# Selective scan on one core: moving two of eight multiplies by the step size from VectorE to GpSimd, through copies by ScalarE

## What is computed

```python
proj = x @ W_x                                  # delta_raw, B_ssm, C_ssm
delta = softplus(delta_raw @ W_dt + b_dt)
A = -exp(A_log)                                 # (128, 16)
dA = exp(einsum('bld,dn->bldn', delta, A))
dBx = einsum('bld,bln->bldn', delta * x, B_ssm)

def step(h, inp):
    dA_t, dBx_t, C_t = inp
    h = dA_t * h + dBx_t
    y_t = einsum('bdn,bn->bd', h, C_t)
    return (h, y_t)
```

## Time and profile before

| what | value |
|---|---|
| median of 3 runs | 2394.18 us (2393.65 to 2394.51) |
| time of the profiled execution | 2391.51 us |
| its span, first to last instruction | 2389.5 us |
| granted TensorE clock over the span | 0.921 |
| busy: TensorE, VectorE, ScalarE, GpSimd | 1911.1, 1571.5, 1375.2, 1019.3 us |

### The profile page before, as it was taken

One profiled execution on the slowest core, in us unless ns is written; L12 is line 12 of the kernel. 1 busy time (PEld: TensorE's weight loads), 2 busy tenths in 40 slices (PEclk: granted clock), 3 DMA queues, 4 the chain that ended last, 5 costly groups with the idle time before them and its releaser, 6 DMA issues. The chain is left out here.

```text
span 2389.5 us, 36303 instructions
## 1 busy us (share of the span) xinstructions
PE 1911.1 (80%) x11731; PEld 865.0 (36%) x11731; DVE 1571.5 (66%) x2373; ACT 1375.2 (58%) x2286; POOL 1019.3 (43%) x1118
## 2 busy tenths in 40 slices
PE   4457886377774765899999999999999966599997
PEld 2113332243453421344444444444444422222222
DVE  4979995786447856777777777777777635511112
ACT  2446662343333334677666676666666533599995
POOL 0156663244004521466666666666666631500001
PEclk9769998589896987999999999999999988899999
DMA  2000000000000001111111111111111100512110
GB/s 87 0 14 0 0 0 0 1 1 1 0 1 0 1 1 52 47 55 54 53 54 56 56 56 56 56 56 56 56 56 56 50 24 8 124 41 52 46 50 36
DMA packets 71431, 84.45 MB, mean 35 GB/s; under 512 B 20545, under 2 KB 44033, under 8 KB 71169
## 3 DMA queue, kind: packets, MB, share of 16 engines
q1 hardware_dynamic: 66224, 79.80, 11.5%
q10 hardware_dynamic: 5040, 2.56, 0.4%
HBM read 71.95 MB, written 9.57 MB: 34 GB/s over the span
## 5 line engine op out<-in xcount | busy, mean ns | idle before, releaser
L1638 DVE SCALAR_TENSOR_TENSOR fu_kv<-fu_ps_kv,fa_vec,fu_kv 128x511 f32<-128x511 f32 x366 | 253.2, 741 | 5.6 <-ACT fu_kv L1568 4.0
L2032 ACT ACTIVATE rt_p<-rt_ps_s 128x1024 f32<-128x1024 f32 x256 | 240.3, 1042 | 25.3 <-PE rt_ps_o L1977 16.5
L1716 POOL TENSOR_TENSOR fu_p<-fu_p 128x768 f32<-128x768 f32 x64 | 116.2, 1816 | 295.2 <-PE fu_ps_n L1413 290.8
L1383 PE MATMUL fu_ps_s<-fu_qn,fu_kn 64*128 64x512 f32 (+3 forms) x1024 | 190.0, 468 | 6.1 <-ACT fu_p L1550 5.5
L1618 DVE TENSOR_REDUCE fu_nm<-fu_ps_m 128x2 f32<-128x1024 f32 x64 | 78.4, 1225 | 176.5 <-PE fu_ps_m L1406 176.5
L602 POOL TENSOR_TENSOR scan_hC<-scan_h,scan_c 128x1024 f32<-128x1024 f32 x64 | 150.7, 2354 | 82.9 <-DVE scan_h L582 82.9
L1413 PE MATMUL fu_ps_n<-fu_p,fu_vt 128*64 128x512 f32 (+3 forms) x1024 | 166.1, 445 | 0.0
L527 PE MATMUL scan_ps_y<-scan_hC,w_ident 128*128 128x512 f32 x256 | 130.3, 632 | 40.9 <-POOL scan_hC L602 24.3
L582 DVE TENSOR_TENSOR_SCAN scan_h<-scan_dA,scan_ps_b 128x1024 f32<-128x1024 f32 x64 | 146.4, 2287 | 2.2
L1977 PE MATMUL rt_ps_o<-rt_p,rt_va 128*32 128x512 f32 x1024 | 137.2, 608 | 10.0 <-ACT rt_p L2032 8.1
L1441 PE MATMUL fu_ps_kv<-w_XN,fa_wp 128*128 128x512 f32 x244 | 122.8, 626 | 17.3 <-DVE fu_cr L1611 15.3
(11 more groups left out here) (353 smaller groups left out, 5071.3 us busy)
## 6 DMA issues: line engine op xcount, KB each, us to landing
fu_rb<-rms_rows SPq DMA_DIRECT2D x256, 128.0 KB, 3.0
fu_ro<-rms_rows SPq DMA_DIRECT2D x128, 128.0 KB, 3.0
ra_stackq<-rope_parts SPq DMA_DIRECT2D x168, 32.0 KB
ra_stackk<-rope_parts SPq DMA_DIRECT2D x168, 32.0 KB
w_X<-in_xT SPq DMA_DIRECT2D x4, 512.0 KB
fa_wp<-in_wp SPq DMA_DIRECT2D x8, 256.0 KB
fu_cr<-ncum_rows SPq DMA_DIRECT2D x128, 3.0 KB
rope_parts<-rp_hi SPq DMA_DIRECT2D x16, 128.0 KB, 2.9
```

The costliest lines, as they stand in the source:

```text
L1383: pe.matmul(sps[:, h, at:at + T - t * P], k[head(h), t * P:(t + 1) * P], q[head(h), t * P:T], start=(at == 0), stop=False)
L1638: dve.scalar_tensor_tensor(acc, projected(a, k)[:, 0:T - j], vec[:, a % GA, at:at + 1], acc, ALU.mult, ALU.add).then_inc(done, 1)
L1716: pool.tensor_tensor(tail, tail, P13[:, :, 0:3 * P], ALU.add).then_inc(s.d1, 1)
L2032: act.activation(pr[k % 2][i][:, :, :], sps[(U * n + u) % RING][:, :, :], ACT.Exp, scale=DH_B ** -0.5).then_inc(s.exp, 1)
```

## The change

Pairs 3 and 7 of each batch are treated apart. TensorE makes their B rows one pair earlier, right before the C of pair 2 (6), and not in bps but in cps, the C buffer. ScalarE copies them from there to a new SBUF tile bsb. GpSimd multiplies bsb by DX into a new tile pb, and this product stands in its order ahead of h times C of pair 1 (5). ScalarE then copies pb into bps[1], between the exponentials and the C copy of pair 3 (7). VectorE runs the recurrence of those pairs from bps as before and makes no multiply for them. The C buffer has ten uses in a batch for eight, the counts waited for change with that, and GpSimd's loop over the batches is unrolled.

```diff
--- before.py
+++ after.py
@@ -497,6 +497,9 @@
         with Stage(nc, "scan") as st:
             PAIRS = N_STATE // 2
             BEHIND = 2
+            APART = (3, 7)
+            NORMAL = PAIRS - len(APART)
+            USES = PAIRS + len(APART)
             selbc = st.sb("selbc", [96, 2 * N_STATE, P], BF16)
             bps = [st.ps(f"b{k}", [P, 2, T]) for k in range(2)]
             cps = st.ps("c", [P, 2, T])
@@ -505,7 +508,17 @@
             hst = [st.sb(f"h{k}", [P, 2, T]) for k in range(2)]
             csb = [st.sb(f"c{k}", [P, 2, T]) for k in range(2)]
             hC = [st.sb(f"hC{k}", [P, 2, T]) for k in range(BEHIND + 2)]
-            s = st.sems("sel zero b c dA dBx scan csb hC sum ysum")
+            bsb, pb = (st.sb(n, [P, 2, T]) for n in ("bsb", "pb"))
+            s = st.sems("sel zero b c dA dBx scan csb hC sum ysum bsb pb put")
+
+            def normal(p):
+
+                return p - sum(a < p for a in APART)
+
+            def use(p):
+
+                return p + sum(a - 1 <= p for a in APART)
+
 
             with st.block() as block:
 
@@ -530,11 +543,17 @@
                     def step(n, last):
                         for p in range(PAIRS):
                             if n is not None:
-                                pe.wait_ge(s.scan, count(n, PAIRS, p - 1))
-                                for j in range(2):
-                                    m = pe.matmul(bps[p % 2][:, j, :], selbc[:, 2 * p + j, :], BC[:, n, :], start=True, stop=True)
-                                m.then_inc(s.b, 1)
-                                pe.wait_ge(s.csb, PAIRS * n + p)
+                                if p not in APART:
+                                    pe.wait_ge(s.scan, count(n, PAIRS, p - 1))
+                                    for j in range(2):
+                                        m = pe.matmul(bps[p % 2][:, j, :], selbc[:, 2 * p + j, :], BC[:, n, :], start=True, stop=True)
+                                    m.then_inc(s.b, 1)
+                                if p + 1 in APART:
+                                    pe.wait_ge(s.csb, USES * n + use(p) - 1)
+                                    for j in range(2):
+                                        m = pe.matmul(cps[:, j, :], selbc[:, 2 * p + 2 + j, :], BC[:, n, :], start=True, stop=True)
+                                    m.then_inc(s.c, 1)
+                                pe.wait_ge(s.csb, USES * n + use(p))
                                 for j in range(2):
                                     m = pe.matmul(cps[:, j, :], selbc[:, N_STATE + 2 * p + j, :], BC[:, n, :], start=True, stop=True)
                                 m.then_inc(s.c, 1)
@@ -558,7 +577,14 @@
                                     k = 2 * p + j
                                     m = act.activation(dA[p % 2][:, j, 1:T], DL[:, n, 1:T], ACT.Exp, scale=w.decay[:, k:k + 1])
                                 m.then_inc(s.dA, 1)
-                                act.wait_ge(s.c, PAIRS * n + p + 1)
+                                if p + 1 in APART:
+                                    act.wait_ge(s.c, USES * n + use(p))
+                                    act.wait_ge(s.pb, len(APART) * n + APART.index(p + 1))
+                                    act.activation(bsb[:, :, :], cps[:, :, :], ACT.Copy).then_inc(s.csb, 1)
+                                if p in APART:
+                                    act.wait_ge(s.pb, len(APART) * n + APART.index(p) + 1)
+                                    act.activation(bps[p % 2][:, :, :], pb[:, :, :], ACT.Copy).then_inc(s.put, 1)
+                                act.wait_ge(s.c, USES * n + use(p) + 1)
                                 act.wait_ge(s.hC, count(n, PAIRS, p - 1))
                                 act.activation(csb[p % 2][:, :, :], cps[:, :, :], ACT.Copy).then_inc(s.csb, 1)
                             if last is not None and p == BEHIND:
@@ -574,9 +600,11 @@
                         dve.memset(dA[k][:, :, 0:1], 0.0).then_inc(s.zero, 1)
 
                     def recur(m, p):
-                        done = PAIRS * m + p + 1
-                        dve.wait_ge(s.dBx, done)
-                        dve.wait_ge(s.dA, done)
+                        if p in APART:
+                            dve.wait_ge(s.put, len(APART) * m + APART.index(p) + 1)
+                        else:
+                            dve.wait_ge(s.dBx, NORMAL * m + normal(p) + 1)
+                        dve.wait_ge(s.dA, PAIRS * m + p + 1)
                         dve.wait_ge(s.hC, count(m, PAIRS, p - 1))
                         flat = [t[p % 2][:, :, :].rearrange("p j t -> p (j t)") for t in (hst, dA, bps)]
                         dve.tensor_tensor_scan(flat[0], flat[1], flat[2], 0.0, ALU.mult, ALU.add).then_inc(s.scan, 1)
@@ -584,10 +612,11 @@
                     def step(n, last):
                         for p in range(PAIRS):
                             if n is not None:
-                                dve.wait_ge(s.b, PAIRS * n + p + 1)
-                                dve.wait_ge(s.scan, count(n, PAIRS, p - 1))
-                                dx = DX[:, n, :].rearrange("p (o t) -> p o t", o=1).broadcast_to([P, 2, T])
-                                dve.tensor_tensor(bps[p % 2][:, :, :], dx, bps[p % 2][:, :, :], ALU.mult).then_inc(s.dBx, 1)
+                                if p not in APART:
+                                    dve.wait_ge(s.b, NORMAL * n + normal(p) + 1)
+                                    dve.wait_ge(s.scan, count(n, PAIRS, p - 1))
+                                    dx = DX[:, n, :].rearrange("p (o t) -> p o t", o=1).broadcast_to([P, 2, T])
+                                    dve.tensor_tensor(bps[p % 2][:, :, :], dx, bps[p % 2][:, :, :], ALU.mult).then_inc(s.dBx, 1)
                                 recur(n, p)
 
                     pipeline(dve, step)
@@ -596,12 +625,19 @@
                 def _(pool):
                     def step(n, last):
                         for p in range(PAIRS if n is not None else 0):
+                            if p + 2 in APART:
+                                k = len(APART) * n + APART.index(p + 2)
+                                pool.wait_ge(s.csb, USES * n + use(p + 1))
+                                pool.wait_ge(s.put, k)
+                                dx = DX[:, n, :].rearrange("p (o t) -> p o t", o=1).broadcast_to([P, 2, T])
+                                pool.tensor_tensor(pb[:, :, :], dx, bsb[:, :, :], ALU.mult).then_inc(s.pb, 1)
                             pool.wait_ge(s.scan, PAIRS * n + p + 1)
-                            pool.wait_ge(s.csb, PAIRS * n + p + 1)
+                            pool.wait_ge(s.csb, USES * n + use(p) + 1)
                             pool.wait_ge(s.sum, count(n, PAIRS, p - BEHIND - 1))
                             pool.tensor_tensor(hC[p % (BEHIND + 2)][:, :, :], hst[p % 2][:, :, :], csb[p % 2][:, :, :], ALU.mult).then_inc(s.hC, 1)
 
-                    pipeline(pool, step)
+                    for n in range(B):
+                        step(n, None)
                     pool.wait_ge(s.hC, PAIRS * B)
 
         with Stage(nc, "ssmo") as st:
```

## The result

| what | before | after |
|---|---|---|
| median, 15 runs each, same chip | 2394.5 us | 2405.2 us |
| ratio, with its 95% interval | | 1.0048 (1.0036 to 1.0059) |
| profiled execution, its span | 2391.5, 2389.5 us | 2409.7, 2407.6 us |
| the scan stage in it | 230.2 us | 240.8 us |

The change costs 10.7 us between the medians (0.45%; 0.48% by the ratio). The stage alone grew by 10.6 us. The profiled execution is 18.2 us longer than that of before; the other 7.6 lie outside the stage, in code that is the same in both. So I explain the stage.

The account below looks back on a forecast made before the run. VectorE alone was taken to set the scan stage's pace. The chain's +1.9 and the +6.7 of TensorE's low clock sum to +8.6 us on the 2394.2 us median, giving 2403 us, range 2387 to 2413.

Parts of the forecast that it names:

- VectorE is relieved but sets the pace no longer: Scan stage: 16 multiplies leave VectorE, at most 19.8 us to win, but its scans then wait for other engines.
- Prices of the added operations: Per operation: GpSimd's new product 2.35 us, ScalarE's copy of B 1.02, its copy of the product into PSUM 1.03.
- The chain of four pairs: TensorE's catching up, B copy, new product and h·C of pair 5: 13.9 us against 13.78; +1.9 us at full clock.
- The saved 1.24 us turn into a wait of 1.1 for GpSimd: VectorE before the scan of pair 7: done at 12.8 us, it gets h·C of pair 5 only at 13.9.
- The sequencers' extra register work: Costed at nothing, with GpSimd's unrolled loop: they run while the engines are busy or waiting.
- The clock, 6 stretches, +6.7: TensorE's lumped idle time brings 6 stretches at 1.2 GHz, about 1.6 us each, less 2.9 now: +6.7 us.
- A quick product: Rival, 12%: GpSimd's new product takes 1.93 us, the chain 13.5 for four pairs, 6.7 less; 2389.5 us, or 2387.
- VectorE stays the pace: Rival, that or half of it 5%: everything else in time, 25.1 us a batch, -19.8, so 2374 us.
- The shared port: Rival, 1%: the new product cannot run beside VectorE's scans or multiplies, 37.6 us more, 2440 us.

Follow-up runs that it names:

- experiments 4: The changed kernel with matmuls that nobody reads put in TensorE's idle gaps; 2387.3 and 2389.0 us, too few executions for a ratio.
- 5: The kernel before with only TensorE's sums moved from two to three pairs behind, nothing of the change in it; 2386.7 us, ratio 0.9977.
- Experiment 3: The changed kernel with TensorE's sums three pairs behind instead of two; 2387.2 us, ratio 0.9967.
- experiment 2: The changed kernel with four h buffers instead of two; 2402.1 us, ratio 1.0037 against the kernel before.
- experiment 6: The changed kernel with sums three pairs behind and VectorE's scan waiting for its own multiply last; 2377.5 us, 0.9928; repeated in another session, 2380.6 us, 0.9941.
- experiment 10: The changed kernel with pair 7 alone treated apart instead of pairs 3 and 7; 2409.5 us, ratio 1.006.
- experiment 8: The kernel of experiment 7 with pairs 2 and 6 treated apart instead of 3 and 7; 2374.9 us, ratio 0.9917.
- experiment 9: The changed kernel without ScalarE's copy of the product back into PSUM, scans of pairs 3 and 7 reading it from SBUF; 2417.6 us, ratio 1.0091.
- experiment 11: The changed kernel with GpSimd's new product made for 32 of each 512 tokens only and unread matmuls filling TensorE's gaps; 2378.2 us, one execution.
- experiment 7: The kernel of experiment 6 with four h and four C buffers instead of two each; 2385.3 us, ratio 0.9961.

## Why the forecast held

Forecast 2403 us against 2405.2, and slower as expected. By its steps:

- **VectorE is relieved but sets the pace no longer.** Right. It lost 16 multiplies and gained 27 us of idle time (15.0 before scans, 12.1 before multiplies).
- **Prices of the added operations.** Right: 2.36, 1.02 and 1.02 us for 2.35, 1.02 and 1.03. The choice that mattered was 2.35 for the product, between 1.93 and 2.81.
- **The chain of four pairs, 13.9 us, +1.9.** Right in size. At the high level the scans of pair 7 of two batches lie 27.83 us apart (293.88 to 321.71), 13.9 for four pairs, and experiments 4 and 5 put the chain at +2.4. Experiment 3 shows where it can be cut: at the sums.
- **"The saved 1.24 us turn into a wait of 1.1 for GpSimd".** Right in the first batch (1.00 to 1.06), not in the loop (0.41 to 0.57): the scans behind a multiply start 1.39 to 1.42 us after it there, for 1.24, which used up the slack first. And the wait is a symptom, as experiment 2 shows.
- **"The sequencers' extra register work ... I cost at nothing".** Wrong in kind. It shows as 40 gaps of 0.19 us, 7.6 us. In the change they lie in slack and cost nothing; once the chain is cut, shortening them is worth 1.9 us (experiment 6).
- **The clock, 6 stretches, +6.7.** Right mechanism, size too small. Eight sums behind the one at the start are long (at 183.49, 201.19, 214.39, 232.09, 245.29, 262.99, 276.13 and 361.01). A ninth, at 378.70, starts with the last scan and delays the end by only some 0.3 us: the last sum ends 2.36 us after its h·C (383.45), for 2.03 in the kernel before. The price was right: a batch with two of them takes 30.9 us against 27.83, so 1.5 each, for 1.6. 8 x 1.5 - 2.9 = +9.1; with the chain 11.0 to 11.5, and the stage grew by 10.6. By experiments 4 and 5 the parts are 8.2 for the clock and 2.4 for the chain. The mis-sized term is the count, carried over as a share of gaps from the kernel before: a share of 3 in 7 was applied to 15 gaps of another shape and order, and 8 of them fell. That it came out near was in part luck, for experiment 10, with half as many copies of B in TensorE's way, has ten.
- **The rivals.** A quick product was priced at -6.7 for 0.42 us less; 2.04 us less gives 7.0 in all, 0.44 per half batch, so the chain has a floor just under it that I did not work out. "VectorE stays the pace" needed another order: experiment 8 has it. The shared port does not bite in this change, because the product goes through PSUM; experiment 9 shows it biting when it does not.

## What to carry to other kernels

Before moving work off the busiest engine, follow the new work through every queue it enters and add up the chain that closes on itself, the catching-up of the other engines included; when it comes out near the old rhythm, the move gains nothing until that chain is cut, here by taking the sums from one pair further back. An accumulation that waits for the freshest product is the first place to cut, since taking it later cost no buffer here and no later end: the stage of before ends 2.7 us after its last h·C, and so does that of experiment 5 (372.38 to 375.05, 369.74 to 372.41). When work goes to GpSimd, keep one input of each VectorE instruction that runs beside it in PSUM, where the trace shows one held up otherwise, as in experiment 9.

## What was unexpected of the hardware

- A scan of 128x1024 takes 2.29 us with one input in PSUM and 4.35 us with both in SBUF beside a GpSimd product: it ends 2.14 to 2.15 us after GpSimd's instruction has ended (experiment 9).
- A register instruction that carries the wait between two dependent VectorE instructions goes with a gap of 0.19 us before the second (40 times, 7.6 us). With that wait behind the others the gap is 0.13, and in the first batch, outside the loop, it grows from 0.03 to 0.13: the order of the waits before one instruction has a price either way.
- Matmuls that nobody reads brought the granted clock of the stage from 0.91 to 0.98 and the stage down by 11.6 us, though TensorE was busy 22.6 us more.
- Outside the stage, in the same instructions, the profiled executions differ by 13 us: from 2155.9 (experiment 11) to 2168.9 (after), with 2161.3 before. What decides it is open, and it blurs every comparison of single executions of this program. Medians have it too: against the kernel before, experiment 6 gains 14.1 us and its repetition 14.9 where the stage gives 9.9 and 9.8, experiment 7 gains 6.3 where the stage gives 11.9, and experiment 9 loses 22.1 where the stage loses 27.7. So a gain of some 5 us of the program can't be put down to the stage by the median alone.
